# First stage of a gated cross-attention and mixture kernel: three fp32 products as high and low halves made by GpSimd, in a new order of steps

## The reference, cut to what matters

```
zn  = layernorm(x)                                       # per token
q   = zn @ Wq + bq     k = ctx @ Wk + bk                 # 16 heads of 16; one k and one v for all heads
v   = ctx @ Wv + bv
att = softmax(q k^T / sqrt(256))                         # 256 tokens x 16 heads x 77 context rows
x   = x + tanh(g) * (att @ v)
xn  = layernorm(layernorm(x)) * gamma + beta
logits = (xn / |xn|) @ (mu / |mu| * scale)               # 256 tokens x 256 slots
dispatch = softmax over experts   combine = softmax over all slots
slot_in  = dispatch^T @ xn
```

## Time and profile before

| | |
|---|---|
| median of 3 runs (lowest to highest) | 1022.22 us (1020.51 to 1024.47) |
| profiled execution, its own time | 1018.67 us |
| its span | 1016.9 us |
| mean granted TensorE clock | 0.985 |
| PE, PEld busy | 945.3 us (93%), 809.0 us (80%) |
| DVE, ACT, POOL busy | 769.9 us (76%), 576.2 us (57%), 398.3 us (39%) |

### The profile page before, as it was taken

One profiled execution on the slowest core, in us unless ns is written; L12 is line 12 of the kernel. 1 busy time (PEld: TensorE's weight loads), 2 busy tenths in 40 slices (PEclk: granted clock), 3 DMA queues, 4 the chain that ended last, 5 costly groups with the idle time before them and its releaser, 6 DMA issues.

```text
span 1016.9 us, 23135 instructions
## 1 busy us (share of the span) xinstructions
PE 945.3 (93%) x6523; PEld 809.0 (80%) x6523; DVE 769.9 (76%) x2336; ACT 576.2 (57%) x1344; POOL 398.3 (39%) x571
## 2 busy tenths in 40 slices
PE   5999999999999878999999999997999995999995
PEld 4666666766766557999999999986898885999995
DVE  3777777777766336788888888889888878888884
ACT  1688888888887633443443444433555542666663
POOL 1011111111111002544453454345675751777776
PEclk9999999999999989999999999999999997999998
DMA  7765765764740250110010001000123545778785
GB/s 219 181 145 127 168 136 115 170 145 108 173 115 1 65 176 28 31 52 27 27 53 27 27 27 54 27 7 1 43 93 113 172 131 177 124 125 134 125 133 69
DMA packets 91812, 98.42 MB, mean 97 GB/s; under 512 B 14992, under 2 KB 85472, under 8 KB 91744
## 3 DMA queue, kind: packets, MB, share of 16 engines
q1 hardware_dynamic: 77504, 79.11, 29.9%
q0 software_dynamic: 13680, 17.84, 10.3%
q10 hardware_dynamic: 560, 0.66, 0.2%
HBM read 30.18 MB, written 59.01 MB: 88 GB/s over the span
## 4 chain that ended last, share of the span: by engine, by line
PE 55%; DVE 6%; issue 1%; POOL 1%; ACT 1%; DMA 0%; POOLq 0%; DVEq 0%; ACTq 0%
PE c_out L1373 3%; PE c_turned L1384 3%; PE c_hidden L1377 3%; PE c_mlp L1377 3%; PE c_hidden L1379 3%; PE c_hidden L1378 3%; PE c_cross L1373 3%; PE c_mlp L1378 3%; PE c_mlp L1379 3%; PE m_gate L2215 3%; PE m_gate L2217 3%; PE m_gate L2216 2%; PE c_scores L1373 2%; PE m_router L2137 1%; PE c_turned L1373 1%; PE m_gate L2160 1%
## 5 line engine op out<-in xcount | busy, mean ns | idle before, releaser
L1720 POOL DMA_INDIRECT out<-early_weights,aim x71 | 110.5, 1556 | 57.1 <-DMA out<-early_weights,aim 27.9
L1189 ACT ACTIVATE f_hidden<-c_hidden,f_b 128x256 f32<-128x256 f32 x128 | 53.7, 471 | 66.6 <-PE c_hidden L1379 66.6
L1377 PE MATMUL c_mlp<-f_w_hi,f_hidden_hi 128*128 128x256 f32 x256 | 80.6, 315 | 7.5 <-DVE f_hidden_lo L1307 7.5
L1695 POOL DMA_INDIRECT sorted_rows<-m_z,slot_i x64 | 69.6, 1088 | 36.4 <-issue 18.5
L1377 PE MATMUL c_hidden<-y2T_hi,f_w_hi 128*128 128x256 f32 x256 | 77.7, 304 | 0.0
L1379 PE MATMUL c_hidden<-y2T_hi,f_w_lo 128*128 128x256 f32 x256 | 72.8, 284 | 0.0
L1378 PE MATMUL c_hidden<-y2T_lo,f_w_hi 128*128 128x256 f32 x256 | 72.7, 284 | 0.0
L1379 PE MATMUL c_mlp<-f_w_hi,f_hidden_lo 128*128 128x256 f32 x256 | 72.4, 283 | 0.0
L1378 PE MATMUL c_mlp<-f_w_lo,f_hidden_hi 128*128 128x256 f32 x256 | 72.3, 283 | 0.0
L784 PE MATMUL ps_probT<-ident,prob 128*77 128x128 f32 x512 | 67.1, 274 | 3.7 <-ACT prob L511 3.2
L628 DVE TENSOR_REDUCE mx<-ps_scores 128x8 f32<-128x616 f32 x64 | 50.9, 795 | 25.4 <-PE ps_scores L714 25.3
(11 more groups left out here) (355 smaller groups left out, 3115.3 us busy)
## 6 DMA issues: line engine op xcount, KB each, us to landing
sorted_rows<-no_row SPq DMA_DIRECT2D x15, 2340.0 KB, 12.2
m_z<-sorted_rows SPq DMA_DIRECT2D x71, 130.0 KB
early_weights<-expert_chunks SPq DMA_DIRECT2D x8, 640.0 KB, 4.6
combT<-combineT_all SPq DMA_DIRECT2D x16, 256.0 KB, 2.3
slT<-slots_all SPq DMA_DIRECT2D x16, 256.0 KB, 2.5
out<-x_all SPq DMA_DIRECT2D x8, 512.0 KB, 6.1
x_all<-x SPq DMA_DIRECT2D x15, 256.0 KB, 11.4
f_w_stage<-L_xattn_w SPq DMA_DIRECT2D x4, 512.0 KB, 3.7
```

What stands on the lines that cost most here:

```text
L1189: last = act.activation(hf[:, q % 2, j, :], psH[:, q % 2, j, :], ACT.Relu, bias=fb1[:, c_:c_ + 1])
L1377: pe.matmul(out, lh, rh, start=start, stop=False, skip_group_check=shared)
L1695: pool.indirect_dma_start(out=sorted_rows[:, :], in_=zn[:, b % 3, t, :], in_offset=None, out_offset=bass.IndirectOffsetOnAxis(ap=slot_i[:, ...
L1720: pool.indirect_dma_start(out=self.out[:, :], in_=xo[:, i % XO, :], in_offset=None, compute_op=ALU.add, out_offset=bass.IndirectOffsetOnAx ...
```

## The change

The products of `queries`, `scores` and `logits` are each replaced by three products of fp32r halves (`mm3`, and the `terms` loop in `scores`). Five new pairs of tiles hold the halves of `zT`, `qT`, `kblock`, `xuT` and, made once, of `wq` and `mu_unit`. POOL makes all of them: a copy that converts, then a subtraction. Where PE waited for ACT's or DVE's tile, it now waits for POOL's halves; ACT and DVE wait with the next batch's tile until POOL has read the old one. The order of the steps is another one; in it, copies u = 0 and u = 2 of the turned exponentials are DVE's (`probT_out`), u = 1 and u = 3 remain ACT's.

```diff
-        order = [(MID, "scores", 0), (MID, "row_max", 0), (MIX, "xuT_out"), (OUT, "values_out", 0), (MID, "scores_out", 0),
...
+        order = [(PRE, "ln1_stats"), (MIX, "turn_xu"), (MIX, "xu_halves"), (MID, "scores", 0), (PRE, "rstd1"),
+                 (MID, "row_max", 0), (MIX, "xuT_out"), (OUT, "probT_act", 3), (OUT, "values_out", 0),
+                 (MID, "scores_out", 0), (PRE, "ln1_mean"), (OUT, "turn_p", 3), (MID, "row_max", 1),
+                 (MID, "scores_out", 1), (OUT, "values", 0), (MIX, "logits_out"), (PRE, "ln1_apply"),
+                 (MIX, "neg_max"), (OUT, "values_out", 1), (MID, "scores", 1), (MIX, "logits"), (MIX, "neg_maxT"),
+                 (MID, "exps", 0), (MIX, "combine"), (OUT, "out_rec", 0), (OUT, "out_scale", 0), (OUT, "out_rec", 1),
+                 (OUT, "values", 1), (OUT, "out_scale", 1), (MIX, "turn_logits"), (MID, "exps", 1),
+                 (OUT, "turn_values", 0), (MIX, "dispatch"), (MIX, "combineT_out"), (MID, "scores", 2),
+                 (PRE, "kv_move"), (MID, "v_load"), (PRE, "zT_out"), (OUT, "turn_values", 1), (MIX, "turn_comb"),
+                 (PRE, "z_halves"), (MIX, "disp_scale"), (MID, "row_max", 2), (PRE, "kv"), (MIX, "normalise"),
+                 (MID, "turn_p", 0), (OUT, "x1"), (MID, "probT_out", 0), (OUT, "ln2_stats"), (PRE, "turn_z"),
+                 (MID, "scores_out", 2), (MID, "turn_p", 1), (OUT, "ln2_mean"), (MIX, "turn_disp"),
+                 (MIX, "disp_out"), (OUT, "rstd2"), (MID, "probT_act", 1), (MID, "exps", 2), (PRE, "kv_out"),
+                 (MID, "scores", 3), (PRE, "k_halves"), (PRE, "q_out"), (MIX, "slots_out"), (OUT, "ln2_center"),
+                 (PRE, "queries"), (MID, "exps", 3), (MIX, "slot_inputs"), (MID, "row_max", 3), (MID, "turn_p", 2),
+                 (PRE, "q_halves"), (MIX, "comb_scale"), (OUT, "squares"), (MID, "scores_out", 3),
+                 (OUT, "ln2_scale"), (OUT, "runit"), (MID, "probT_out", 2)]
...
+            pool.wait_ge(const_in.sem, 16)
+            alone(pool)
+            pool.tensor_copy(wq_h[:], wq).then_inc(wq_split.sem, 1)
+            pool.wait_ge(wq_split.sem, 1)
+            pool.tensor_tensor(wq_l[:], wq, wq_h[:].bitcast(F32), ALU.subtract).then_inc(wq_split.sem, 1)
+
+            def halves(b, high, low, whole, split):
+                pool.tensor_copy(high[:], whole[:]).then_inc(split.sem, 1)
+                need(pool, split, b, 1)
+                pool.tensor_tensor(low[:], whole[:], high[:].bitcast(F32), ALU.subtract).then_inc(split.sem, 1)
+
+            def z_halves(b):
+                need(pool, zt_ev, b)
+                reuse(pool, q_mm, b)
+                alone(pool)
+                halves(b, zT_h, zT_l, zT, z_split)
...
             def zT_out(b):
                 need(act, zt_mm, b)
-                reuse(act, q_mm, b)
+                reuse(act, z_split, b)
...
+            def mm3(out, lh, ll, rh, rl, start, stop):
+
+                pe.matmul(out, lh, rh, start=start, stop=False)
+                pe.matmul(out, lh, rl, start=False, stop=False)
+                return pe.matmul(out, ll, rh, start=False, stop=stop)
...
             def queries(b):
-                need(pe, zt_ev, b)
+                need(pe, z_split, b)
...
-                        last = mm(psA[:, m * S:(m + 1) * S], wq[:, k, m * P:(m + 1) * P], zT[:, k, :], k == 0, k == KD - 1)
+                        last = mm3(psA[:, m * S:(m + 1) * S], wq_h[:, k, cols], wq_l[:, k, cols], zT_h[:, k, :], zT_l[:, k, :],
+                                   k == 0, k == KD - 1)
...
-                    need(pe, q_ev, b)
-                    need(pe, kb_done, b)
+                    need(pe, q_split, b)
+                    need(pe, k_split, b)
...
-                for h in range(2):
-                    rows = slice(h * P // 2, (h + 1) * P // 2)
-                    last = mm(psS[:, h, 0:UG // 2 * L], qT[rows, chunk, tile * P:(tile + 1) * P],
-                              kblock[rows].rearrange("p g l -> p (g l)"))
+                terms = ((qT_h, kb_h), (qT_h, kb_l), (qT_l, kb_h))
+                for n, (q, k) in enumerate(terms):
+                    for h in range(2):
+                        rows = slice(h * P // 2, (h + 1) * P // 2)
+                        last = mm(psS[:, h, 0:UG // 2 * L], q[rows, chunk, tile * P:(tile + 1) * P],
+                                  k[rows].rearrange("p g l -> p (g l)"), n == 0, n == len(terms) - 1)
...
             def logits(b):
-                need(pe, xut_ev, b)
+                need(pe, xu_split, b)
...
-                        last = mm(psL[:, t, :], xuT[:, k, t * P:(t + 1) * P], mu_unit[:, k, :], k == 0, k == KD - 1)
+                        last = mm3(psL[:, t, :], xuT_h[:, k, cols], xuT_l[:, k, cols], mu_h[:, k, :], mu_l[:, k, :], k == 0, k == KD - 1)
```

More of the change, by code:

```diff
@@ L263, in phase_a @@
         mu_unit = sb("mu_unit", [P, KD, SLOTS])
+        mu_h, mu_l = sb("mu_unit_hi", [P, KD, SLOTS], F32R), sb("mu_unit_lo", [P, KD, SLOTS], F32R)
+        wq_h, wq_l = sb("wq_hi", [P, KD, D], F32R), sb("wq_lo", [P, KD, D], F32R)
+        zT_h, zT_l = sb("zT_hi", [P, KD, S], F32R), sb("zT_lo", [P, KD, S], F32R)
+        qT_h, qT_l = sb("qT_hi", [P, KD, S], F32R), sb("qT_lo", [P, KD, S], F32R)
+        xuT_h, xuT_l = sb("xuT_hi", [P, KD, S], F32R), sb("xuT_lo", [P, KD, S], F32R)
+        kb_h, kb_l = sb("kblock_hi", [P, UG // 2, L], F32R), sb("kblock_lo", [P, UG // 2, L], F32R)
         ctxT = sb("ctx_turned", [P, KD, P])
@@ L339, in phase_a @@
         PRE, MID, OUT, MIX = range(4)
-        order = [(MID, "scores", 0), (MID, "row_max", 0), (MIX, "xuT_out"), (OUT, "values_out", 0), (MID, "scores_out", 0),
[L342 to L351, removed]
-                 (MID, "exps", 2), (MID, "probT_act", 1), (PRE, "q_out"), (MID, "v_load"), (MID, "turn_p", 1),
-                 (PRE, "queries"), (MIX, "slots_out"), (MID, "exps", 3), (MID, "probT_act", 2), (OUT, "runit"),
-                 (MIX, "slot_inputs"), (MID, "scores_out", 3), (OUT, "ln2_center"), (OUT, "squares"), (PRE, "kv_out"),
-                 (MIX, "comb_scale"), (OUT, "ln2_scale"), (MID, "turn_p", 2)]
@@ L422, in _, with q_halves, k_halves, xu_halves @@
             alone(pool)
+            pool.wait_ge(const_in.sem, 16)
[12 more added lines that the diff above has]
+                halves(b, zT_h, zT_l, zT, z_split)
+            def q_halves(b):
+                need(pool, q_ev, b)
+                reuse(pool, sc_mm, b)
+                alone(pool)
+                halves(b, qT_h, qT_l, qT, q_split)
+            def k_halves(b):
+                need(pool, kb_done, b)
+                reuse(pool, sc_mm, b)
+                alone(pool)
+                halves(b, kb_h, kb_l, kblock, k_split)
+            def xu_halves(b):
+                if isinstance(b, int) and b == 0:
+                    pool.wait_ge(mu_done.sem, 1)
+                    pool.tensor_copy(mu_h[:], mu_unit[:]).then_inc(mu_split.sem, 1)
+                    pool.wait_ge(mu_split.sem, 1)
+                    pool.tensor_tensor(mu_l[:], mu_unit[:], mu_h[:].bitcast(F32), ALU.subtract).then_inc(mu_split.sem, 1)
+                need(pool, xut_ev, b)
+                reuse(pool, lg_mm, b)
+                alone(pool)
+                halves(b, xuT_h, xuT_l, xuT, xu_split)
             def rstd1(b):
@@ L453, in runit @@
                 pool.tensor_tensor(ru[:], ru[:], self.minus_half[:, 0:TT], ALU.pow).then_inc(ru_step.sem, 1)
-            run(pool, order, dict(rstd1=rstd1, v_load=v_load, rstd2=rstd2, runit=runit), NB)
+            run(pool, order, dict(z_halves=z_halves, q_halves=q_halves, k_halves=k_halves, xu_halves=xu_halves, rstd1=rstd1, v_load=v_load, rstd2=rstd2, runit=runit), NB)
         @block.scalar
@@ L474, in q_out @@
                 need(act, q_mm, b)
-                reuse(act, sc_mm, b)
+                reuse(act, q_split, b)
                 for k in range(KD):
@@ L751, in queries @@
             def queries(b):
-                need(pe, zt_ev, b)
+                need(pe, z_split, b)
+                if isinstance(b, int) and b == 0:
+                    need(pe, wq_split, b)
                 for m in range(KD):
+                    cols = slice(m * P, (m + 1) * P)
                     for k in range(KD):
-                        last = mm(psA[:, m * S:(m + 1) * S], wq[:, k, m * P:(m + 1) * P], zT[:, k, :], k == 0, k == KD - 1)
+                        last = mm3(psA[:, m * S:(m + 1) * S], wq_h[:, k, cols], wq_l[:, k, cols], zT_h[:, k, :], zT_l[:, k, :],
+                                   k == 0, k == KD - 1)
                 last.then_inc(q_mm.sem, 1)
```

7 lines of the change are left out of this document (5 added, 2 removed).

## The result

| | before | after |
|---|---|---|
| median (lowest to highest) | 1021.62 us (1020.51 to 1024.47, 4 runs) | 1064.83 us (1064.42 to 1072.14, 4 runs) |
| profiled execution, its span | 1018.67, 1016.9 | 1064.98, 1063.2 |
| PE, DVE busy | 945.3, 769.9 us | 943.3, 827.2 us |
| ACT, POOL busy | 576.2, 398.3 us | 551.1, 514.6 us |
| a full turn of the first stage | 19.27 us | 21.1 us |

The changed kernel is slower: ratio 1.0431, 95% interval 1.0406 to 1.0456. Nearly all of it lies in the first stage: the first expert product, which comes behind it, starts at 342.69 before and at 385.86 after, 43.2 us later. The spans of the two profiled executions differ by 46.3 us; the other 3.1 fall behind that product, in stages that the change leaves alone, and were not followed. The medians differ by 43.2.

A forecast was written before the change was run, and what follows sets the result against it. TensorE sets the 19.27 us turn; with POOL's halves it grows by 1.6 to 20.9. The 13 full turns add 21 and partial turns 12: 33 on 1018.67 is 1052, own range 1042 to 1062, wide range 1018 to 1066.

The forecast's parts named there:

- What PE gains: First stage on PE: queries to 1.50, logits to about 1.65, scores to 0.65 if paired; 0.8 us less work a turn.
- POOL's prices: Halves on POOL: conversion 0.61, subtraction 1.29, kblock's halves some 1.3; POOL goes from 3.06 to 10.3 us a turn.
- The collision: POOL's subtraction of q holds up DVE's ln2_scale, which ends at 3.95 instead of 2.98 after queries' end.
- Everything queued behind turn_xu starts 0.7 to 0.8 later: On PE, scores 0, turn_p 3 and values 0 start 0.7 to 0.8 later than q's halves would allow.
- The other chain of the forecast: After ln2_scale, runit stands ahead of xu_halves on POOL, so logits can start only at 8.3 after queries' end.
- z's halves are there at 19.35: Before queries: PE ends scores 3 at 18.5 at best and waits for z's halves until 19.35; turn 20.9.
- Moving two copies from ACT to DVE doesn't save it: Two 1.0 us copies move: no saving, as ACT waited on PE and DVE rises to some 16.5 us plus delays.
- The forecast's own sign of being wrong: Forecast wrong if the turn is under 19.5, the subtraction under 1 us, or PE's waits on POOL under 0.3 each.
- The partial turns: First and last turns of the first stage, chains without cover: together they add 12 us.
- (a): Rival, 20%: slower without the collision, DVE goes first and POOL waits; a turn of 20.3, +25, 1044.
- (b): Rival, 14%: faster, TensorE stays the bound, POOL's subtraction costs 0.61 for 1.29; 1011.
- (d): Rival, 9%: much slower; 64-row fp32r products run singly, 0.45 more per scores, 1074, or the clock falls at similar price.

The follow-up runs named there:

- order alone: The kernel before, fp32 products and no halves, given the changed kernel's order of steps with its two copies on DVE: 1050.84 us, ratio 1.0279.
- the one tried: The changed kernel with one PE step moved, turn_p 0 ahead of kv instead of behind it: 1080.12 us, ratio 1.0547.

## Why the forecast came out right, and where its steps failed

The direction held, and the range from 1018 to 1066 took in the measured 1065 by 1 us. The forecast's own range, 1042 to 1062, did not, and the loss was 43 us where 33 were forecast. A full turn was forecast at 20.9 and measured at 21.1, which is partly luck, as the steps show:

- **What PE gains: right.** `queries` 1.53 (1.50 forecast), `logits` 1.63 (150.76 to 152.39; 1.65), `scores` 0.62 to 0.63 where no wait follows (0.65): the 64-row products run in pairs. The kernels show 0.90 a turn between fp32 and fp32r in one order (0.8).
- **POOL's prices: right.** 0.61 and 1.27 (0.61, 1.29), `kblock` 0.45 + 0.85 (1.3), 10.12 us a turn (10.3).
- **The collision: right, and shown by taking it away.** `xn` ended 3.85 behind the end of `queries` (165.90 + 1.75 is 167.65, less 163.80; forecast 3.95). `turn_xu` started 3.98 behind (4.0). Without q's subtraction `xn` takes 0.88 and the turn loses 0.71.
- **"Everything queued behind turn_xu starts 0.7 to 0.8 later": wrong in its consequence.** Moving `turn_xu` changed the turn by 0.03 at most. The other chain of the forecast, `xn`, `runit`, `xu_halves`, `logits`, is the one that counts: `logits` started 8.07 behind the end of `queries` (8.3), 0.06 after its halves.
- **"z's halves are there at 19.35": the number right, its role wrong.** They were there at 19.29 (161.98 less 142.69), but `queries` started at 19.58, bound by PE's own queue. The step that failed is the sentence before: "the end of `scores` 3 at 18.5 at best". I had put 0.5 on the waits of the stretch up to `turn_z`, where the row shows 0.39 ahead of `kv`, and none behind it, where it shows 1.06 ahead of `turn_p` 1. `turn_z` ended at 16.4 (16.35). "Moving two copies from ACT to DVE doesn't save it" looked at DVE's total and not at who needs copy 0: the next `turn_p`.
- **So the attribution fell.** The forecast gave the turn's 1.6 us to the halves' round trips and none to the order. The runs give 1.73 to the order and, net, 0.1 to the halves: their subtractions (+1.0) eat what PE gains (-0.9). The missed wait before `turn_p` 1 and the halves of z, expected to be the last to come, lay side by side and ended within 0.3 of each other; that they came to the same sum is luck.
- **The forecast's own sign of being wrong came true.** It named waits of PE on POOL under 0.3 each as such a sign. In the full turns they were 0.14 ahead of `logits` and none ahead of `queries`. The sum came out, the mechanism of z's round trip did not.
- **The partial turns: mis-sized.** Forecast 12 (6 at either end), measured 19 (43.2 less 13 turns of 1.84). From the first to the last `slot_inputs` and its two ends:

| | first slot_inputs | 12 full turns | last 3 |
|---|---|---|---|
| before | 64.51 | 231.3 | 43.2 |
| order alone | +5.4 | +20.8 | +2.7 |
| changed order, no subtractions | +7.3 | +9.9 | +2.8 |
| without q's subtraction | +11.0 | +13.4 | +6.7 |
| after | +15.0 | +21.8 | +6.4 |

The last three were 6.4 (6 forecast). The first column holds the three partial turns and most of one full turn; it is 15 where I had 6.5 and up to 1.6, so 8. The halves give 9.6 of it and the order 5.4, for which there was no term. Nor was there one for the clock in the fill, some 5 us by the estimate above. From 20 to 80 us the order alone and the kernel without any subtractions ran at 1.00 as before, and without q's subtraction the clock fell once, from 61.0 to 64.4.

Of the rivals, (a) had no collision and (b) a subtraction at 0.61; the rows decide against both. (d)'s single products did not occur. The clock stayed at 1.00 in the full turns; it fell in the first turns, at a quarter of (d)'s price. The one run of 1072.14 had a mean clock of 0.975, the three near 1064.7 had 0.980 to 0.982.

What stays open: PE's busy time is 0.4 a turn higher in this order with the same fp32 products (19.08, 18.68). The rows say in which groups, not why; which neighbours on PE make a step longer was not tried. Nor is it shown which single cover would bring the order back to 19.3: the one tried made room at one wait and opened three.

## What to carry to other kernels

In a pipeline that one list orders, cost a reordering by itself first, in the old arithmetic: for each round trip out of an engine, write down which steps of that engine lie between, and compare with the trip; a copy of 1.2 us behind a step of 0.5 is a wait, whatever else is saved. Price the fill by itself too: there the round trips are bare, and in this kernel the clock fell behind them. Halves of a product were cheaper here on the engine that already copies the value out of PSUM than on a third one with a hand-over more. And look whether large two-input work on POOL runs where DVE's two-input step is the path: here that cost 0.7 us a turn.
